# Last stage of a graph network block on one core: another order of gates, shared layer and expert outputs, roots as a power on GpSimd, stores from SP

## The chip, the cores and the metric

The kernel runs on one core of a Trainium2 chip. The time is device microseconds of that core for one whole execution. The core's engines are TensorE (PE in the profile, its weight loads PEld), VectorE (DVE), ScalarE (ACT), GpSimd (POOL) and SP, which here only issues DMAs. Each engine works through its own list of instructions in order; semaphores are the only order between them. TensorE has a granted clock of two levels, 1.2 and 2.4 GHz (0.50 and 1.00 in the profile).

## The reference, cut to what matters

There are 6250 nodes with 256 values and 206250 edges. `xn` is the layer norm of x. A transformer convolution over the edges (8 heads) gives `out`; what follows is per node, and is what the changed stage computes:

```
x_r  = xn @ Wskip.T + bskip
beta = sigmoid(concat[out, x_r, out - x_r] @ Wbeta.T)
y    = layernorm(xn + beta * x_r + (1 - beta) * out) * g1 + b1'
t    = x + layernorm(y + gelu(y @ W1.T + b1) @ W2.T + b2) * g2 + b2'     # W1: 256 -> 1024
m    = layernorm(t)
shared = relu(relu(m @ sW1 + sb1) @ sW2 + sb2) @ sW3 + sb3               # 256, 128, 256
expert_e = relu(relu(m @ eW1 + eb1) @ eW2 + eb2) @ eW3 + eb3             # 4 experts: 128, 64, 256
w    = softmax over the two largest of softmax(m @ gW + gb), else 0
result = t + shared + sum_e w_e * expert_e
```

Everything is fp32. A layer norm divides by sqrt(var + 1e-5).

## The kernel before, in words

Two stages come ahead: projections of all nodes, and the long loop over the edges (until about 2848 us). The diff touches only the last stage, from line 997 on.

**Tiling.** The nodes are 49 blocks of 128 rows. They go through the stage in 13 parts: part 0 has three blocks, parts 1 to 11 have four, part 12 has two (`parts`, `wd`; NS is 13). Hidden layers are computed with features on the partitions and up to 512 nodes as columns (`hidden`, into two PSUM buffers `hid`, which ScalarE empties with gelu or relu). What must come back with nodes on the partitions is computed block by block (`node_major`, 256 columns, into three PSUM buffers `nat`, which VectorE empties). Transposes of the node rows (`transpose_rows`) go through two PSUM buffers `tr`, which ScalarE copies to `rT`.

**Steps.** TensorE's list is a loop over steps s, written out by hand. In step s it does, before the change: W1 of part s (eight `hidden`, and between the fifth and the sixth the transposes of m of part s-1), gate logits and first shared layer of part s-1, W2 of part s, then of part s-1 the first expert layers (e1), the second shared layer (s2) and the second expert layers (e2), the transposes of y of part s+1 and of x of part s+2, the outputs of part s-1 (per block one shared and four expert `node_major`), and `skip` of part s+2. The buffers `hid`, `nat` and `tr` are used in turn, so every engine must take them in the same order; the list `order` numbers them.

**VectorE's list in step s:** `after_attention(s+1)` (the sum for beta, then the sigmoid, first layer norm, y), `gates(s-1)`, `divide_by_sum(s+2)`, `add_ffn(s)` (takes W2's blocks), `after_ffn(s)` (two layer norms; gives t and m, in `mb`), `combine(s-1)` (takes the outputs, five operations per block), `skip_less_out(s+2)` (takes the skip blocks).

**ScalarE's list in step s:** the eight gelus of W1, with exp(-z) of part s+1 behind the third, the copies of the transposes of m behind the fifth, and one root behind the sixth; relus of the first shared layer; two exponentials of the gates; relus of e1 with one root behind the second; s2, e2; copies of the transposes of y and x; one root. A root is exp(-0.5 * ln(var + eps)), two activations of one column per block, each with a load of its function table.

**Other queues.** SP loads `xnb` three parts ahead and `xb` one part ahead, each behind the semaphore that says that the buffer is free. GpSimd issues the stores of `accb` when `combine` is done; the next `combine` waits for the store.

In VectorE's `layernorm` (L1195 to L1207) the statistics are followed by `var_ready`, then a wait for two signals of ScalarE (`rstd_ready`), then the scaling on L1205. Lines in the profile: L1447 is the matmul in `hidden`, L1454 that in `node_major`, L1438 a transpose, L1480 the gate logits; L1385 the activations of hidden layers, L1374 and L1376 the two of a root, L1367 exp(-z), L1380 the gates' exponentials; on VectorE L1198 batch statistics, L1225 `skip_less_out`, L1234 to L1254 `after_attention` (L1234 its first product, L1239 the first operation behind exp(-z)), L1262 `add_ffn`, L1284 the first and L1290 the first operation behind an exponential in `gates`, L1321 and L1326 `combine`.

Of the kernel before, what the change touches and what calls it, by code (L numbers as in the profile page):

```python
# [45 lines left out]
def build(nc, a, out):  # L46
# [75 lines left out]
    with top:  # L122
# [875 lines left out]
        with ExitStack() as s3:  # L998

            W = 4
# [12 lines left out]
            tb = [sbt(s3, f"tb{i}", [P, W, D]) for i in range(2)]  # L1015
# [29 lines left out]
            eps3 = sbt(s3, "eps3", [P, 1])  # L1045
# [5 lines left out]
            lv3 = sbt(s3, "lv3", [P, W])  # L1051
            rs3 = sbt(s3, "rs3", [P, W])
            zb = sbt(s3, "zb", [P, W])
# [7 lines left out]
            we = sbt(s3, "we", [P, W, NE])  # L1061
# [10 lines left out]
            for s in range(NS + 1):  # L1072
                order += [("w1", s), ("r2", s - 1), ("s1", s - 1), ("w2", s), ("e1", s - 1), ("s2", s - 1), ("e2", s - 1),
                          ("r1", s + 1), ("r0", s + 2), ("out", s - 1), ("skip", s + 2)]
# [12 lines left out]
            ws_landed, w3_landed, consts3, rows_set = sem("ws_landed"), sem("w3_landed"), sem("consts3"), sem("rows_set")  # L1087
# [10 lines left out]
            with nc.Block() as block:  # L1098
                @block.sync
                def _(sp):  # L1100
# [39 lines left out]

                    for dst, src in loads[:NW3S]:
                        sp.dma_start(dst, src).then_inc(ws_landed, 16)
# [32 lines left out]
                def _(dve):  # L1175
# [414 lines left out]
```

## Time and profile before

| | us |
|---|---|
| median of three runs (3913.5 to 3918.82) | 3915.66 |
| the profiled execution | 3916.25 |
| its span, first to last instruction | 3914.2 |
| of the span, the last stage | from about 2848 on |
| TensorE busy over the span | 3539.5 (90%) |
| VectorE, ScalarE, GpSimd busy | 1990.8, 1675.7, 2048.3 |

The profile is one execution. A timeline row has the start and the time of one or several like instructions on one engine, its source line, the operation, the tile written and those read, and in brackets the idle time ahead of it with what ended it. An fp32 matmul shows as two records on PE. Ends of matmuls are modelled, so a start minus the next start is the better measure. A row of the busy table gives a stretch and its length, then for PE, PEld, DVE, ACT and POOL the busy us with the number of instructions, then the granted clock, the share of the DMA engines and GB/s. A stage's time on the path is read from TensorE's starts; busy shares over the whole span mix three stages with different limits.

### The profile page before, as it was taken

The page shows a single profiled execution, that of the slowest core. Times are in us where ns is not written, and L with a number is a line of the kernel's source. Part 1 is how long each engine was busy: PE and PEld are TensorE (multiplying, and loading weights), DVE is VectorE, ACT ScalarE, POOL GpSimd, SP SyncE. Part 2 cuts the span into 40 slices and gives each one's busy share as a digit, 9 for nine tenths or more (in the row PEclk, how much of TensorE's full clock was granted, in tenths as well). Part 3 has the DMA queues.
Part 4 walks back from the last instruction along what each step waited for, and adds up shares of the span by engine and source line. Part 5 has one row for each costly group of instructions (what it writes and reads, how often), then busy time and mean ns, then how long its engine had stood idle before and what let it go on. Part 6 is the DMA issues. An engine that isn't in the chain of part 4 may idle for free. (4 is left out here: it accounts for less than half of the span.)

```text
span 3914.2 us, 77635 instructions
## 1 busy us (share of the span) xinstructions
PE 3539.5 (90%) x22914; PEld 2185.8 (56%) x22914; DVE 1990.8 (51%) x5550; ACT 1675.7 (43%) x3636; POOL 2048.3 (52%) x2100
## 2 busy tenths in 40 slices
PE   5879999999999999999999999999948898898988
PEld 2445555555555555555555555555535555555645
DVE  6344444544454554454554454454456555555553
ACT  2234444444444444444444444444424434334342
POOL 3067777777777777777777777777700000000000
PEclk9979999999999999999999999999978888888887
DMA  6467777777777777777777777777620000000000
GB/s 206 162 162 197 192 194 196 198 196 195 195 197 195 196 196 198 197 196 197 198 202 194 195 196 194 198 196 198 159 77 21 22 17 22 17 22 20 11 14 14
DMA packets 637776, 572.41 MB, mean 146 GB/s; under 512 B 430486, under 2 KB 523991, under 8 KB 637700
## 3 DMA queue, kind: packets, MB, share of 16 engines
q0 software_dynamic: 159616, 429.57, 37.1%
q1 hardware_dynamic: 478100, 142.10, 17.3%
q8 instruction: 30, 0.49, 0.1%
q14 instruction: 30, 0.25, 0.0%
HBM read 632.99 MB, written 33.05 MB: 170 GB/s over the span
## 5 line engine op out<-in xcount | busy, mean ns | idle before, releaser
L610 POOL DMA_INDIRECT F<-kv_rows,srcg x1970 | 1996.6, 1014 | 689.0 <-issue 595.9
L686 DVE COPY PT<-pPT 128x384 f32<-128x384 f32 x393 | 219.2, 558 | 1139.6 <-PE pPT L876 1137.3
L883 PE MATMUL pZ<-F,PT 128*64 128x320 f32 x4704 | 744.7, 435 | 0.0
L856 PE MATMUL ring<-ident,F 128*128 128x128 f32 x3940 | 605.3, 285 | 130.6 <-ACT FT L788 122.1
L856 PEld LDWEIGHTS ring<-ident,F 128*128 128x128 f32 x3940 | 418.6, 141 | 417.4 <-ACT FT L788 215.1
L788 ACT ACTIVATE FT<-ring 128x512 f32<-128x512 f32 (+1 forms) x1182 | 579.1, 525 | 68.2 <-PE ring L856 10.3
L794 ACT ACTIVATE Pw<-pS,nMn 128x384 f32<-128x384 f32 x393 | 226.8, 577 | 870.8 <-DVE nMn L681 832.9
L1168 POOL DMA_DIRECT2D out_dram<-accb x13 | 9.8, 750 | 1046.5 <-DVEq L1330 1046.5
L883 PEld LDWEIGHTS pZ<-F,PT 128*64 128x64 f32 x4704 | 368.4, 136 | 253.7 <-issue 1.8
L869 PE MATMUL pS<-F,G 80*64 80x320 f32 x1572 | 299.4, 459 | 0.0
L866 PE MATMUL pS<-FT,qh 128*32 128x320 f32 x3144 | 294.1, 446 | 1.2 <-issue 0.7
L674 DVE TENSOR_SCALAR F<-F,nid 16x640 f32<-16x640 int32 x394 | 245.1, 622 | 19.2 <-issue 1.3
L680 DVE TENSOR_REDUCE nmx<-pS 128x1 f32<-128x384 f32 x393 | 219.2, 558 | 56.8 <-PE pS L869 50.7
L832 ACT ACTIVATE Zs<-pZ 128x320 f32<-128x320 f32 x392 | 171.3, 437 | 170.4 <-PE pZ L883 163.2
L1454 PE MATMUL nat<-eW,e 65*128 65x256 f32 x392 | 168.0, 598 | 63.2 <-DVE accb L1321 63.2
L896 PE MATMUL pZv<-ident,Zs 128*128 128x64 f32 x1568 | 218.2, 262 | 0.0
L876 PE MATMUL pPT<-ident,Pw 128*128 128x128 f32 x1179 | 215.4, 292 | 0.8 <-ACT Pw L794 0.8
L889 PE MATMUL pM<-ident,F 64*128 64x64 f32 x1965 | 206.3, 233 | 0.0
L896 PEld LDWEIGHTS pZv<-ident,Zs 128*128 128x128 f32 x1568 | 205.9, 192 | 0.0
L1385 ACT ACTIVATE h<-hid,b1c 128x512 f32<-128x512 f32 (+2 forms) x104 | 66.2, 661 | 299.8 <-PE hid L1447 299.5
L869 PEld LDWEIGHTS pS<-F,G 80*64 80x64 f32 x1572 | 77.9, 135 | 204.8 <-issue 204.8
L806 ACT ACTIVATE G<-pM 64x512 f32<-64x512 f32 x99 | 58.5, 591 | 310.9 <-PE pM L846 310.9
(214 smaller groups left out, 4477.8 us busy)
## 6 DMA issues: line engine op xcount, KB each, us to landing
F<-in_edge_attrT SPq DMA_DIRECT2D x788, 80.0 KB
F<-kv_rows,srcg POOLq DMA_INDIRECT x1970
F<-in_dst SPq DMA_DIRECT2D x788, 20.0 KB
srci<-src_front SPq DMA_DIRECT2D x796, 1.5 KB, 3.2
kv_rows<-kvs SPq DMA_DIRECT2D x7, 1792.0 KB, 6.7
qb<-q_cols SPq DMA_DIRECT2D x100, 64.0 KB
U<-in_x SPq DMA_DIRECT2D x7, 896.0 KB, 10.9
xn_rows<-xs SPq DMA_DIRECT2D x7, 896.0 KB, 6.7
```

The source lines that it names most:

```text
L610: pool.indirect_dma_start(out=F[s][:, t, 0:KV], out_offset=None, in_=kv_d, in_offset=bass.IndirectOffsetOnAxis(ap=srcg[j % GB][:, col:col ...
L674: dve.tensor_scalar(F3[j][DE:K3, :], F3[j][DE:K3, :].bitcast(I32), nid[DE:K3, c], None, ALU.not_equal).then_inc(neq_done, 1)
L680: ch.step(dve.tensor_reduce(nmx[:, j:j + 1], pS[:, 0:SW], AX.X, ALU.max, negate=True))
L686: dve.tensor_copy(PT[:, :, :], pPT[:, 0:SW].rearrange("p (t r) -> p t r", r=P)).then_inc(pt_emptied, 1)
L788: act.activation(FT[j % 2][:, :, t0 * P:t1 * P], ring[n % 2][:, 0:KD * w].rearrange("p (k e) -> p k e", e=w), ACT.Copy).then_inc(ring_empt ...
L794: act.activation(Pw[:, :], pS[:, 0:SW], ACT.Exp, bias=nMn[:, j:j + 1], accum_out=lsum[:, j:j + 1]).then_inc(p_done, 1)
L856: m = pe.transpose(ring[n % 2][:, k * w + (t - t0) * P:k * w + (t - t0 + 1) * P], F[j][:, t, k * P:(k + 1) * P], ident[:, :])
L866: pe.matmul(pS[r:r + C, o * HP:o * HP + OW], qh[half][:, c, g + o, :], FT[j % 2][:, c, o * OW:(o + 1) * OW], start=True, stop=False)
L869: m = pe.matmul(pS[o * HP:(o + 1) * HP, o * HP:o * HP + OW], G3[half][0:K3, g + o, :, :].rearrange("p c r -> p (c r)"), F3[s][0:K3, o * OW ...
L876: m = pe.transpose(pPT[:, t * P:(t + 1) * P], Pw[:, t * P:(t + 1) * P], ident[:, :])
L883: m = pe.matmul(pZ[rows, 0:ZW], PT[:, t, rows], F[s][:, o * TO + t, D:FP], start=(t == 0), stop=(t == KB - 1))
L896: pe.matmul(pZv[:, g].rearrange("p (o c r) -> p o c r", o=2, c=KD)[:, :, c, :], Zs[:, c * P:(c + 1) * P], ident[:, :].rearrange("p (o c r) ...
```

## The change

- TensorE's step becomes: W1 of part s with the transposes of m of part s-1 inside, gate logits and first shared layer of part s-1, W2 of part s, transposes of y (s+1) and x (s+2), **outputs of part s-2**, `skip` (s+2), and then e1, s2, e2 of part s-1. There are NS + 2 steps in place of NS + 1.
- VectorE: `gate_sum`, the first half of `after_attention`, becomes a function of its own and moves behind `skip_less_out`; `combine(s-2)` stands behind `add_ffn(s)`; `after_ffn(s)` moves to the end of the step. Each `layernorm` gets one more operation, var + eps.
- The roots are one `tensor_tensor` with `ALU.pow` and a tile of -0.5 on GpSimd. ScalarE has no roots any more, and exp(-z) moves to the end of its step.
- The stores are issued by SP, between the loads of `xnb` and `xb`.
- `tb` has three buffers in place of two, `we` two in place of one.

```diff
@@ -1069,9 +1069,9 @@
             tr_at, hid_at, nat_at = {}, {}, {}
             nt = nh = nn = 0
             order = [("r0", 0), ("skip", 0), ("r0", 1), ("skip", 1), ("r1", 0)]
-            for s in range(NS + 1):
-                order += [("w1", s), ("r2", s - 1), ("s1", s - 1), ("w2", s), ("e1", s - 1), ("s2", s - 1), ("e2", s - 1),
-                          ("r1", s + 1), ("r0", s + 2), ("out", s - 1), ("skip", s + 2)]
+            for s in range(NS + 2):
+                order += [("w1", s), ("r2", s - 1), ("s1", s - 1), ("w2", s), ("r1", s + 1), ("r0", s + 2), ("out", s - 2),
+                          ("skip", s + 2), ("e1", s - 1), ("s2", s - 1), ("e2", s - 1)]
             for name, p in order:
                 if 0 <= p < NS:
                     if name in ("r0", "r1", "r2"):
...
@@ -1138,6 +1139,21 @@
                             sp.wait_ge(x_used, p)
                         sp.dma_start(xb[:, 0:t1 - t0, :], x_d[:, t0:t1, :]).then_inc(xb_landed, 16)
 
+                    stored = [0]
+
+                    def store(p):
+                        t0, t1 = parts[p]
+                        sp.wait_ge(out_ready, p + 1)
+                        whole = min(t1, N // P) - t0
+                        last = min(t1 * P, N) - (t0 + whole) * P
+                        if whole:
+                            stored[0] += 1
+                            sp.dma_start(out[t0 * P:(t0 + whole) * P, :].rearrange("(j p) d -> p j d", p=P), accb[:, 0:whole, :]
+                                         ).then_inc(out_stored, 16)
+                        if last:
+                            stored[0] += 1
+                            sp.dma_start(out[(t0 + whole) * P:N, :], accb[0:last, whole, :]).then_inc(out_stored, 16)
+
                     for dst, src in loads[:NW3S]:
                         sp.dma_start(dst, src).then_inc(ws_landed, 16)
                     load_xn(0)
@@ -1146,36 +1162,43 @@
                         sp.dma_start(dst, src).then_inc(w3_landed, 16)
                     load_x(0)
                     load_xn(2)
-                    for s in range(NS):
+                    for s in range(NS + 2):
                         if s + 3 < NS:
                             load_xn(s + 3)
+                        if s >= 2:
+                            store(s - 2)
                         if s + 1 < NS:
                             load_x(s + 1)
+                    sp.wait_ge(out_stored, 16 * stored[0])
 
                 @block.gpsimd
                 def _(pool):
                     pool.memset(tri[:, :, :], 1.0).then_inc(consts3, 1)
                     pool.wait_ge(consts3, 1)
+                    pool.memset(half[:, :], -0.5).then_inc(half_set, 1)
+                    pool.wait_ge(half_set, 1)
 
                     pool.affine_select(out=tri[:, :, :], in_=tri[:, :, :], compare_op=ALU.is_ge, fill=0.0, base=-1,
                                        pattern=[[1, NE], [-1, NE]], channel_multiplier=0).then_inc(consts3, 1)
 
-                    for p, (t0, t1) in enumerate(parts):
-                        pool.wait_ge(out_ready, p + 1)
-                        whole = min(t1, N // P) - t0
-                        last = min(t1 * P, N) - (t0 + whole) * P
-                        if whole:
-                            pool.dma_start(out[t0 * P:(t0 + whole) * P, :].rearrange("(j p) d -> p j d", p=P), accb[:, 0:whole, :]
-                                           ).then_inc(out_stored, 16)
-                        if last:
-                            pool.dma_start(out[(t0 + whole) * P:N, :], accb[0:last, whole, :]).then_inc(out_stored, 16)
-                    pool.wait_ge(out_stored, 16 * (NS - 1 + (whole > 0) + (last > 0)))
+                    lns = [0]
+
+                    def rstd(p):
+                        lns[0] += 1
+                        pool.wait_ge(var_ready, lns[0])
+                        pool.tensor_tensor(rs3[:, 0:wd[p]], vr3[:, 0:wd[p]], half[:, 0:wd[p]], ALU.pow).then_inc(rstd_ready, 1)
+
+                    rstd(0)
+                    for s in range(NS):
+                        if s + 1 < NS:
+                            rstd(s + 1)
+                        rstd(s)
+                        rstd(s)
 
                 @block.vector
                 def _(dve):
                     ch = Chain(dve, "dve3")
 
-                    dve.memset(eps3[:, :], LN_EPS).then_inc(rows_set, 1)
                     dve.memset(e2[EH2:EH2 + 1, :, :], 1.0).then_inc(rows_set, 1)
                     dve.wait_ge(ws_landed, 16 * NW3S)
                     dve.wait_ge(consts3, 2)
@@ -1198,9 +1221,10 @@
                             s = dve.bn_stats(st3[:, j, :], src[:, j, :])
                         ch.step(s)
                         mean_and_var(dve, ch, st3[:, 0:w, :], mn3[:, 0:w], vr3[:, 0:w], D)
+                        ch.step(dve.tensor_scalar(vr3[:, 0:w], vr3[:, 0:w], LN_EPS, None, ALU.add))
                         dve.sem_inc(var_ready, 1)
                         lns[0] += 1
-                        dve.wait_ge(rstd_ready, 2 * lns[0])
+                        dve.wait_ge(rstd_ready, lns[0])
                         for j in range(w):
                             s = dve.tensor_scalar(dst[:, j, :], src[:, j, :], mn3[:, j:j + 1], rs3[:, j:j + 1],
                                                   ALU.subtract, ALU.mult)
@@ -1225,16 +1249,22 @@
                             dve.tensor_sub(d[:, j, :], nat[n % NATS][:, 0:D], d[:, j, :]).then_inc(nat_emptied, 1)
                         dve.wait_ge(nat_emptied, nat_at["skip", p] + wd[p])
 
-                    def after_attention(p):
+                    def gate_sum(p):
 
                         w, d = wd[p], db[p % 3]
-                        ob, x, t, y = weighted(p)[:, :, :, 0:C], xnb[p % 2], ta[:, 0:w, :], yb[:, 0:w, :]
+                        ob, t, y = weighted(p)[:, :, :, 0:C], ta[:, 0:w, :], yb[:, 0:w, :]
                         if p >= 1:
                             dve.wait_ge(tr_filled, tr_at[1, p - 1] + wd[p - 1])
                         ch.step(dve.tensor_tensor(heads(t), ob, heads(wide(w12, w)), ALU.mult))
                         ch.step(dve.tensor_tensor(y, d[:, 0:w, :], wide(w23, w), ALU.mult))
                         ch.step(dve.tensor_add(t, t, y))
                         dve.tensor_reduce(zb[:, 0:w], t, AX.X, ALU.add).then_inc(z_ready, 1)
+                        dve.wait_ge(z_ready, p + 1)
+
+                    def after_attention(p):
+
+                        w, d = wd[p], db[p % 3]
+                        ob, x, t, y = weighted(p)[:, :, :, 0:C], xnb[p % 2], ta[:, 0:w, :], yb[:, 0:w, :]
                         dve.wait_ge(ez_ready, p + 1)
                         ch.step(dve.tensor_scalar(ezb[:, 0:w], ezb[:, 0:w], 1.0, None, ALU.add))
                         ch.step(dve.reciprocal(ezb[:, 0:w], ezb[:, 0:w]))
...
@@ -1331,28 +1361,31 @@
 
                     divide_by_sum(0)
                     skip_less_out(0)
+                    gate_sum(0)
                     after_attention(0)
                     divide_by_sum(1)
                     skip_less_out(1)
-                    for s in range(NS + 1):
+                    gate_sum(1)
+                    for s in range(NS + 2):
                         if s + 1 < NS:
                             after_attention(s + 1)
-                        if s >= 1:
+                        if 1 <= s <= NS:
                             gates(s - 1)
                         if s + 2 < NS:
                             divide_by_sum(s + 2)
                         if s < NS:
                             add_ffn(s)
-                            after_ffn(s)
-                        if s >= 1:
-                            combine(s - 1)
+                        if s >= 2:
+                            combine(s - 2)
                         if s + 2 < NS:
                             skip_less_out(s + 2)
+                            gate_sum(s + 2)
+                        if s < NS:
+                            after_ffn(s)
 
                 @block.scalar
                 def _(act):
-                    act.wait_ge(rows_set, 2)
-                    lns = [0]
+                    act.wait_ge(rows_set, 1)
 
                     def transposed(r, p):
 
...
@@ -1385,49 +1409,42 @@
                         act.activation(dst[0:rws, k, 0:w], hid[n % 2][0:rws, 0:w], func, bias=bias[0:rws, k:k + 1]).then_inc(hid_emptied, 1)
 
                     transposed(0, 0)
+                    exp_z(0)
                     transposed(0, 1)
-                    exp_z(0)
-                    rstd(0)
                     transposed(1, 0)
+                    exp_z(1)
                     act.wait_ge(w3_landed, 16 * (NW3 - NW3S))
                     for s in range(NS + 1):
                         c = s - 1
                         if s < NS:
                             for k in range(KH):
                                 hidden("w1", s, k, h1, ACT.Gelu, b1c)
-                                if k == 2 and s + 1 < NS:
-                                    exp_z(s + 1)
                                 if k == 4 and c >= 0:
                                     transposed(2, c)
-                                if k == 5 and s + 1 < NS:
-                                    rstd(s + 1)
-                        elif c >= 0:
+                        else:
                             transposed(2, c)
                         if c >= 0:
                             for k in range(KD):
                                 hidden("s1", c, k, sh1, ACT.Relu, sb1c)
                             exp_gates(c, 0)
                             exp_gates(c, 1)
-                            for e in range(NE):
-                                hidden("e1", c, e, e1, ACT.Relu, eb1c)
-                                if e == 1 and s < NS:
-                                    rstd(s)
-                            hidden("s2", c, 0, sh2[:, None, :], ACT.Relu, sb2c)
-                            for e in range(NE):
-                                hidden("e2", c, e, e2, ACT.Relu, eb2c, EH2)
-                        elif s < NS:
-                            rstd(s)
                         if s + 1 < NS:
                             transposed(1, s + 1)
                         if s + 2 < NS:
                             transposed(0, s + 2)
-                        if s < NS:
-                            rstd(s)
+                        if c >= 0:
+                            for e in range(NE):
+                                hidden("e1", c, e, e1, ACT.Relu, eb1c)
+                            hidden("s2", c, 0, sh2[:, None, :], ACT.Relu, sb2c)
+                            for e in range(NE):
+                                hidden("e2", c, e, e2, ACT.Relu, eb2c, EH2)
+                        if s + 2 < NS:
+                            exp_z(s + 2)
 
                 @block.tensor
                 def _(pe):
                     pe.wait_ge(ws_landed, 16 * NW3S)
-                    pe.wait_ge(rows_set, 2)
+                    pe.wait_ge(rows_set, 1)
 
                     def transpose_rows(r, p, src):
                         for j in range(wd[p]):
...
@@ -1507,7 +1524,20 @@
                             pe.wait_ge(hid_emptied, hid_at["w1", s] + KH)
                             for j in range(wd[s]):
                                 node_major(nat_at["w2", s] + j, [(h1[:, k, j * P:(j + 1) * P], W2T[:, k, :]) for k in range(KH)])
-                        if c >= 0:
+                        if s + 1 < NS:
+                            rows_of_y(s + 1)
+                        if s + 2 < NS:
+                            rows_of_x(s + 2)
+                        if o >= 0:
+                            pe.wait_ge(hid_emptied, hid_at["e2", o] + NE)
+                            for j in range(wd[o]):
+                                cols, n = slice(j * P, (j + 1) * P), nat_at["out", o] + j * (1 + NE)
+                                node_major(n, [(sh2[:, cols], sW3[:, :])])
+                                for e in range(NE):
+                                    node_major(n + 1 + e, [(e2[:, e, cols], eW3[:, e, :])])
+                        if s + 2 < NS:
+                            skip(s + 2)
+                        if 0 <= c < NS:
                             for e in range(NE):
                                 hidden("e1", c, e, P, [(eW1[:, i, e, :], rT[2][:, i, 0:wc]) for i in range(KD)])
                             pe.wait_ge(hid_emptied, hid_at["s1", c] + KD)
@@ -1515,19 +1545,6 @@
                             for e in range(NE):
                                 pe.wait_ge(hid_emptied, hid_at["e1", c] + e + 1)
                                 hidden("e2", c, e, EH2, [(eW2[:, e, :], e1[:, e, 0:wc])])
-                        if s + 1 < NS:
-                            rows_of_y(s + 1)
-                        if s + 2 < NS:
-                            rows_of_x(s + 2)
-                        if c >= 0:
-                            pe.wait_ge(hid_emptied, hid_at["e2", c] + NE)
-                            for j in range(wd[c]):
-                                cols, n = slice(j * P, (j + 1) * P), nat_at["out", c] + j * (1 + NE)
-                                node_major(n, [(sh2[:, cols], sW3[:, :])])
-                                for e in range(NE):
-                                    node_major(n + 1 + e, [(e2[:, e, cols], eW3[:, e, :])])
-                        if s + 2 < NS:
-                            skip(s + 2)
 
 
 NW3, NW3S = 26, 10

```

## Rows read from the trace of the kernel before

**Rows 1.** Busy table of the last stage: from:to, length, each engine's busy us (instructions), clock.

```profile
2900.00:3914.00 1014.00, 878.18 (x2794) 562.45 (x2792) 569.02 (x1385) 403.53 (x635) 10.36 (x14) 0.85 0.06 18
```

**Rows 2.** Timeline of TensorE over one full step: start, us, engine, line, what.

```profile
3186.76 8.75 PE L1447 MATMUL hid<-rT,W1T 128*128 128x512 f32 x20
...
3197.77 5.32 PE L1447 MATMUL hid<-rT,W1T 128*128 128x512 f32 x12
...
3202.93 1.84 PE L1480 MATMUL pg<-gW,rT 128*128 128x4 f32 x16
...
3205.56 5.40 PE L1447 MATMUL hid<-rT,sW 128*128 128x512 f32 x8 [0.79 <-ACT h L1385]
...
3210.79 13.98 PE L1454 MATMUL nat<-W2T,h 128*128 128x256 f32 x64
...
3224.61 7.03 PE L1447 MATMUL hid<-rT,eW 128*128 128x512 f32 x16
...
3232.78 1.95 PE L1447 MATMUL hid<-sh,sW 128*128 128x512 f32 x4 [1.14 <-ACT e L1385]
...
3238.48 0.66 PE L1438 MATMUL tr<-ident,yb 128*128 128x128 f32 x4
...
3242.03 0.60 PE L1454 MATMUL nat<-sW,sh 128*128 128x256 f32 x2
...
3248.92 2.08 PE L1454 MATMUL nat<-eW,e 65*128 65x256 f32 x4 [5.44 <-DVE accb L1321]
...
3263.59 5.36 PE L1454 MATMUL nat<-WskT,rT 128*128 128x256 f32 x16
...
3268.78 3.60 PE L1447 MATMUL hid<-rT,W1T 128*128 128x512 f32 x8
```

**Rows 3.** Timeline of VectorE in the same step and the next.

```profile
3213.24 0.17 DVE L1290 TENSOR_REDUCE gs<-gx 128x4 f32<-128x16 f32 x1 [3.92 <-ACT gx L1380]
...
3219.99 0.76 DVE L1262 TENSOR_TENSOR tb<-nat,db 128x256 f32<-128x256 f32 x2
...
3225.26 1.40 DVE L1198 BATCH_NORM_STATS2 st<-tb 128x6 f32<-128x256 f32 x4
...
3232.09 1.38 DVE L1205 TENSOR_SCALAR db<-tb,mn,rs 128x256 f32<-128x256 f32 x4 [4.01 <-ACT rs L1376]
...
3245.77 1.38 DVE L1205 TENSOR_SCALAR mb<-tb,mn,rs 128x256 f32<-128x256 f32 x4 [5.57 <-ACT rs L1376]
...
3269.44 1.23 DVE L1234 TENSOR_TENSOR ta<-U,w 128x1024 f32<-128x1024 f32 x1
...
3276.37 0.17 DVE L1239 TENSOR_SCALAR ezb<-ezb 128x4 f32<-128x4 f32 x1 [1.93 <-ACT ezb L1367]
...
3285.56 1.38 DVE L1205 TENSOR_SCALAR db<-ta,mn,rs 128x256 f32<-128x256 f32 x4 [2.88 <-ACT rs L1376]
...
3290.76 0.17 DVE L1284 TENSOR_TENSOR g<-pg,rows 128x16 f32<-128x16 f32 x1
```

**Rows 4.** Busy table of two stretches inside expert outputs.

```profile
3252.00:3256.00 4.00, 4.00 (x11) 3.12 (x10) 2.25 (x5) 0.00 (x0) 0.00 (x0) 0.50 0.00 0
...
3904.00:3909.00 5.00, 4.70 (x20) 2.97 (x19) 4.14 (x9) 0.00 (x0) 0.00 (x0) 1.00 0.00 0
```

**Rows 5.** Timeline of VectorE in the outputs of the last part.

```profile
3905.04 2.04 DVE L1326 SCALAR_TENSOR_TENSOR accb<-nat,we,accb 128x256 f32<-128x256 f32 x4
```

**Rows 6.** GpSimd's groups of instructions over the whole span.

```profile
L315 POOL MEMSET U<- 128x1848 f32 x7 | 11.3, 1638 | 57.0 <-DVE xs L354 56.5 <-POOL posb L309 0.5
...
L283 POOL TENSOR_SCALAR_AFFINE_SELECT selh<-selh 128x4 f32<-128x4 f32 x32 | 6.1, 190 | 5.0 <-POOL selh L283 0.5
```

**Rows 7.** Timeline of TensorE, W1 of parts 0, 2 and 11.

```profile
2898.85 2.82 PE L1447 MATMUL hid<-rT,W1T 128*128 128x384 f32 x8 [0.57 <-ACT rT L1362]
...
3022.30 8.75 PE L1447 MATMUL hid<-rT,W1T 128*128 128x512 f32 x20
...
3757.73 9.19 PE L1447 MATMUL hid<-rT,W1T 128*128 128x512 f32 x20
```

More of the change, by code:

```diff
@@ L1014, in build @@
             db = [sbt(s3, f"db{i}", [P, W, D]) for i in range(3)]
-            tb = [sbt(s3, f"tb{i}", [P, W, D]) for i in range(2)]
+            tb = [sbt(s3, f"tb{i}", [P, W, D]) for i in range(3)]
             yb = sbt(s3, "yb", [P, W, D])
@@ L1050, in build @@
             vr3 = sbt(s3, "vr3", [P, W])
-            lv3 = sbt(s3, "lv3", [P, W])
             rs3 = sbt(s3, "rs3", [P, W])
+            half = sbt(s3, "half", [P, W])
             zb = sbt(s3, "zb", [P, W])
@@ L1060, in build @@
             rank = sbt(s3, "rank", [P, W, NE])
-            we = sbt(s3, "we", [P, W, NE])
+            we = [sbt(s3, f"we{i}", [P, W, NE]) for i in range(2)]
             NATS = 3
@@ L1085, in build @@
                         nh += {"w1": KH, "s1": KD, "s2": 1, "e1": NE, "e2": NE}[name]
-            ws_landed, w3_landed, consts3, rows_set = sem("ws_landed"), sem("w3_landed"), sem("consts3"), sem("rows_set")
+            ws_landed, w3_landed, consts3, rows_set, half_set = (
+                sem("ws_landed"), sem("w3_landed"), sem("consts3"), sem("rows_set"), sem("half_set"))
             xn_landed = [sem(f"xn_landed3{i}") for i in range(2)]
@@ L1256, in add_ffn @@
                     def add_ffn(p):
-                        d, t = db[p % 3], tb[p % 2]
+                        d, t = db[p % 3], tb[p % 3]
                         for j in range(wd[p]):
@@ L1265, in after_ffn @@
                     def after_ffn(p):
-                        w, dd, tt = wd[p], db[p % 3], tb[p % 2]
+                        w, dd, tt = wd[p], db[p % 3], tb[p % 3]
                         d, t = dd[:, 0:w, :], tt[:, 0:w, :]
@@ L1307, in gates @@
                         dve.wait_ge(ge_ready, 2 * p + 2)
-                        ch.step(dve.tensor_tensor(we[:, tt, :], gx[:, tt, :], rank[:, tt, :], ALU.mult))
-                        ch.step(dve.tensor_reduce(gs[:, tt], we[:, tt, :], AX.X, ALU.add))
+                        ch.step(dve.tensor_tensor(we[p % 2][:, tt, :], gx[:, tt, :], rank[:, tt, :], ALU.mult))
+                        ch.step(dve.tensor_reduce(gs[:, tt], we[p % 2][:, tt, :], AX.X, ALU.add))
                         ch.step(dve.reciprocal(gs[:, tt], gs[:, tt]))
-                        ch.step(dve.tensor_tensor(we[:, tt, :], we[:, tt, :], four(gs), ALU.mult))
+                        ch.step(dve.tensor_tensor(we[p % 2][:, tt, :], we[p % 2][:, tt, :], four(gs), ALU.mult))
                     def combine(p):
-                        t = tb[p % 2]
+                        t = tb[p % 3]
                         if p >= 1:
@@ L1489, in _ @@
                     pe.wait_ge(w3_landed, 16 * (NW3 - NW3S))
-                    for s in range(NS + 1):
-                        c = s - 1
+                    for s in range(NS + 2):
+                        c, o = s - 1, s - 2
                         if s < NS:
@@ L1498, in _ @@
                                     rows_of_m(c)
-                        elif c >= 0:
+                        elif c < NS:
                             rows_of_m(c)
-                        if c >= 0:
+                        if 0 <= c < NS:
                             wc = wd[c] * P
@@ L1509, in _ @@
                                 node_major(nat_at["w2", s] + j, [(h1[:, k, j * P:(j + 1) * P], W2T[:, k, :]) for k in range(KH)])
-                        if c >= 0:
+                        if s + 1 < NS:
[11 more added lines that the diff above has]
+                            skip(s + 2)
+                        if 0 <= c < NS:
                             for e in range(NE):
```

11 lines of the change are left out of this document (1 added, 10 removed).

## Prediction, made before the kernel after was run

> **What bounds the kernel now.** I read the busy shares by stretch first, then TensorE's timeline of one step of the last stage, then VectorE's beside it, then the granted clock. The change leaves everything up to 2848 us alone; the last stage is the 1014 us of [rows 1], with TensorE busy 878 us of it at a mean granted clock of 0.85. So there are two losses: waits, and time at 1.2 GHz. [Rows 2] are TensorE's starts in one full step. W1 of the next step begins 3268.78 - 3186.76 = 82.0 us after W1 of this one. The largest wait is 5.44 us before the second expert output: PSUM buffers come free only when `combine` starts, and `combine` stands on VectorE behind the whole of `after_ffn`, which itself waited 4.01 and 5.57 us for ScalarE's roots [rows 3]. After that gap the clock is 0.50 although TensorE is busy 4.00 of 4.00 us [rows 4], and stays there through the outputs into `skip`: from 3248.92 to 3263.59 us 14.7 us for outputs whose matmuls take half of that at 2.4 GHz. TensorE is the engine that binds; the chain of a step runs over it, with VectorE and ScalarE only at the gaps.
>
> **The change on TensorE.** I rebuild a step from its starts, all at the full clock. One fp32 matmul shows as two records; a W1 record takes (3202.93 - 3197.77)/12 = 0.43 us, a W2 record (3224.61 - 3210.79)/64 = 0.216 us [rows 2].
> - W1: 32 x 0.43 = 13.8. Gate logits 1.84. First shared layer 8 x 0.43 = 3.4 (5.23 now: half of it ran at half clock, after 2.6 us of gate logits and idling). W2 13.8.
> - Transposes of y and x: 3242.03 - 3238.48 = 3.55 for 8 tiles; those of m, 4 tiles at that rate, 1.8.
> - e1, s2, e2: 3238.48 - 3224.61 = 13.9, less the 1.14 us wait for ScalarE, which stood on two table loads for a root; these go. 12.7.
> - Outputs: VectorE limits them at full clock. The last part shows it: four weighted sums in 2.04 us [rows 5] and one addition of about 0.4, 2.46 per block, 9.8 for four.
> - `skip`: 16 records x 0.216 = 3.5.
> Sum 64.2 us. No matmul is added or dropped: the same parts pass through once, in 15 steps instead of 14. I add 1.0 us, half of the 1.8 us that the first shared layer loses when the clock falls ahead of it; it may still fall there in some steps. 65.2 against 82.0.
>
> **Does VectorE keep up?** Its order becomes: rest of `after_attention`, gates, `divide_by_sum`, `add_ffn`, `combine` (two parts back), `skip_less_out`, `gate_sum`, `after_ffn`. What was never on the path is now near it: `m_ready`. Let 0 be the end of `skip` on TensorE and X the time from variance to root on GpSimd, both handoffs included. `gate_sum` begins at 0.66 and takes 4 x 1.26 = 5.0. `after_ffn` took 3245.77 - 3225.26 = 20.5 us to its last scaling, 9.6 of it the two waits [rows 3]; with that scaling (1.4) and two added eps additions (0.2 each) it is 12.7 + 2X. So m is ready at 18.4 + 2X. TensorE asks for it after e1 to e2 and five eighths of W1, at 12.7 + 8.6 = 21.3. It is in time while X is below 1.5.
> Then one 1.26 addition, `after_attention` (3290.76 - 3276.37 = 14.4, less its 2.88 wait, plus 0.2 = 11.7, plus X): gates start at 31.4 + 3X. They need the exponentials, which came 3213.24 - 3210.79 = 2.45 us after the first shared layer ended; that end is now at 12.7 + 13.8 + 1.8 + 1.8 + 3.4 = 33.5, so 36.0; from there to the first W2 addition 3219.99 - 3213.24 = 6.75, and 0.45 for it: 43.2. TensorE needs this buffer for the fourth W2 block at 33.5 + 10.4 = 43.9. Also in time, with 0.7 us to spare. `combine` finds VectorE free when the outputs begin. Both margins are thin, both hang on X.
>
> **X.** No row shows a power on GpSimd. From below: its small one-input operations take 0.19 us [rows 6], with two handoffs some 0.3. From above: the largest computing operation of GpSimd there is 1.64 us for 1848 columns [rows 6]; the wait that is removed was 2.88 to 5.57 with table loads [rows 3], and a root could be dearer than either. I take 1.0 for four columns, nearer to the small rows, and keep 0.3 to about 7 as bounds. The Trainium skill (GPSIMD Engine Reference, Performance versus the Vector engine) puts a two-input operation at 1.96 times VectorE's; by it this one would be some 0.35 us, an estimate, but the page prices an addition, not a power. The same page (Instruction dispatch) says that the first call of newly loaded code costs about 6 us: that would make 3723 of the time below; no row here shows it.
>
> **The other parts.** ScalarE: three roots a step, each with two loads of its table, leave it; the loads that remain stand beside TensorE. exp(-z) moves to the end of a step, where z has been ready since `gate_sum`: nothing waits. It also stands no longer in W1, so the transposes of m find ScalarE free. SP: a store takes POOL's place, behind the load of xn (asked for at the start of the step) and ahead of the load of x, whose buffer comes free only after `after_ffn`, later than `combine`: the store delays nothing, and the next `combine` asks for it a whole step later. These cost nothing; if a store did hold the x load, a step of slack is there. The third `tb` and second `we` only hold values longer.
>
> **Ends of the stage.** Head, W1 of part 0 to W1 of part 2: 3022.30 - 2898.85 = 123.5 now [rows 7]. New: W1, W2, transposes, skip for three blocks and for four, and part 0's layers (by the numbers above, three quarters for three blocks; no outputs yet) are 77.4; plus 5 for ScalarE, which now waits for z of part 1 before its first gelu; plus 8 for m of part 0 (TensorE gets there after only 8.6 us of W1, VectorE needs 5.0 + 9.7 + 2X = 16.7); plus 4 for the half clock behind that. 94.4; gain 29, most of it the first outputs, which come later. Middle, steps 2 to 10: 3757.73 - 3022.30 = 735.4 now; new 9 x 65.2 = 586.8, less 2.5 (outputs of a part of three blocks), less 2.6 (part 12 has two), plus 2.3 (m late once): 584.0; gain 151. Tail: 3914.2 - 3757.73 = 156.5 now; new 58.1 (step 11, little to transpose or skip) + 43.4 (step 12) + 24.8 (step 13: 19.8 of work and 5 for the last gates ahead of `combine`) + 4.9 (last outputs) + 4.7 (store, as now) + 2 = 137.9; gain 19.
> Together 199: span 3914.2 - 199 = 3715. The profiled execution took 3916.25 us, 2.0 more than its span, and the three runs have a median of 3915.66; I forecast 3717.
>
> **Rivals.**
> A, the clock stays at 1.2 GHz in the outputs. Ahead of them stand transposes in bursts, and at full clock TensorE pauses at each output for VectorE (0.43 of work in 0.5). If it falls there, it stays, as it did although TensorE was fully busy [rows 4]: 14.7 + 2.1 for the first two against 9.8, some 7.2 per step, 87 in all: 3804. Against it: the last part's outputs ran at 1.00 throughout, paused by VectorE in just this way [rows 4, 5]. The page TensorE: Matmul & The Clock Gate of the Trainium skill (A second HAM failure mode) says that small idles between groups, as PSUM banks are cycled, make the clock oscillate: that speaks for A. The same page (Part 1) has sustained activity release the throttle, by which the outputs now should not have stayed slow; the measurement decides, they did.
> B, the root costs 1.5 to 5 us. At 3 us m is 3.1 late and the W2 buffer another 1.5: 4.6 per step, 55 in all, some more in the head: 3775.
> C, slower than before: the same root, dearer. At X = 7 m is 11.1 late, the buffer (39.5 + 3X against 43.9 plus that wait) another 5.5, and an idle of this length leaves the last three eighths of W1 at half clock, 12 x 0.43 = 5.2 more: 87.0 per step, 5.0 over now, about 3975. It decides from X = 5.7. For it: GpSimd computes almost nothing in this kernel, so nothing bounds it from its own rows; against: four columns.
> D, the order does not do what it says: the outputs find their buffers free, but another handoff that I hold for hidden (x copies, y) takes the wait, and only the roots' loads and a few us a step are won: 3850.
>
> **How the numbers follow.** Forecast 0.55, A 0.15, B 0.19, C 0.05, D 0.06. The range 3685 to 3805 takes in the forecast, B and A; its lower end is mine without the additions of 1.0 per step and half of the head's waits. A change within 0.2% (8 us) is what a measurement cannot tell from none; only between C and D does it fall there, 0.01. Faster 0.94, slower 0.05.
>
> **What would show it.** W1 starts 64 to 66 us apart, no gap of 5 us before the outputs, granted clock near 1.0 in them, 2.5 us per block; transposes of m without a wait of more than 0.5 us; GpSimd's power under 1.2 us. It is wrong if TensorE waits for `mb`, if the output blocks take 4.27 us, or if the W2 blocks wait for VectorE.

## The result and the profile after

The kernel after took 3708.0 us (3707.56 to 3708.03, three runs) against 3915.66: 0.947 of before, 95% interval 0.945 to 0.949. Its profiled execution has a span of 3705.8 us. The forecast was 3717 in a range of 3685 to 3805. Two of the sets of runs below were taken while the stage over the edges took some 1000 us more in every kernel (the kernel before: medians of 5019 and 4975 us, mean granted clock 0.83 in place of 0.95); the kernels in them are compared by the length of the last stage in their profiles, first transposes of x to the end, which is 1046.0 us before and 836.9 after.

TensorE's timeline of one full step, in the columns of [rows 2]:

```profile
3185.22 8.83 PE L1464 MATMUL hid<-rT,W1T 128*128 128x512 f32 x20
3193.88 0.60 PE L1455 MATMUL tr<-ident,mb 128*128 128x128 f32 x4
3195.10 0.71 PE L1455 MATMUL tr<-ident,mb 128*128 128x128 f32 x4 [0.61 <-ACT rT L1395]
3195.65 5.32 PE L1464 MATMUL hid<-rT,W1T 128*128 128x512 f32 x12
3200.80 1.84 PE L1497 MATMUL pg<-gW,rT 128*128 128x4 f32 x16
3202.50 3.68 PE L1464 MATMUL hid<-rT,sW 128*128 128x512 f32 x8
3206.02 13.98 PE L1471 MATMUL nat<-W2T,h 128*128 128x256 f32 x64
3219.83 0.60 PE L1455 MATMUL tr<-ident,yb 128*128 128x128 f32 x4
...
3223.12 0.60 PE L1471 MATMUL nat<-sW,sh 128*128 128x256 f32 x2
...
3232.69 3.69 PE L1471 MATMUL nat<-WskT,rT 128*128 128x256 f32 x16
3236.22 7.03 PE L1464 MATMUL hid<-rT,eW 128*128 128x512 f32 x16
...
3248.74 8.82 PE L1464 MATMUL hid<-rT,W1T 128*128 128x512 f32 x20
```

From W1 to W1 it is 3248.74 - 3185.22 = 63.5 us, against 82.0 in [rows 2]. The 5.44 us ahead of the outputs are gone, the first shared layer takes 3206.02 - 3202.50 = 3.5 in place of 5.2, and the outputs 3232.69 - 3223.12 = 9.6. Before they took 3263.59 - 3242.03 = 21.6 with the gap, 14.7 of it behind the gap at half clock. VectorE and GpSimd beside it:

```profile
3191.04 1.01 POOL L1189 TENSOR_TENSOR rs<-vr,half 128x4 f32<-128x4 f32 x1 [8.49 <-DVEq L1225]
```

```profile
3192.09 1.38 DVE L1229 TENSOR_SCALAR mb<-tb,mn,rs 128x256 f32<-128x256 f32 x4 [1.18 <-POOL rs L1189]
...
3215.27 0.76 DVE L1292 TENSOR_TENSOR tb<-nat,db 128x256 f32<-128x256 f32 x2
```

A root costs VectorE 1.18 us where it waited 5.57 for the same one in [rows 3]. (The 5.57 were not all roots: the variance was ready at 3240.2, and ScalarE, still busy with copies of transposes, began the root's first table load at 3242.63.) m is ready at 3192.09 + 1.38 = 3193.47 us and TensorE takes it at 3193.88: 0.4 us of margin. The busy table answers to [rows 1] and [rows 4]: the whole last stage, a stretch in the outputs of a full step, and one in the last outputs but one.

```profile
2900.00:3705.00 805.00, 765.43 (x2789) 472.30 (x2788) 570.95 (x1422) 247.37 (x448) 37.02 (x38) 0.98 0.07 22
3224.00:3232.00 8.00, 8.00 (x35) 5.21 (x33) 7.54 (x17) 0.00 (x0) 0.00 (x0) 1.00 0.00 0
3674.00:3682.00 8.00, 8.00 (x22) 6.13 (x21) 4.91 (x12) 0.00 (x0) 0.00 (x0) 0.55 0.00 1
```

TensorE was busy 878 of 1014 us at 0.85 and is now busy 765 of 805 us at 0.98: the matmuls are the same, so the 113 us less of busy time went with the clock, and the other 96 are waits. The third row is read below, at the ends of the stage.

### The profile page after: what moved, and what is told of

Its sections match the earlier page's. It is cut to its first block and busy times, and to the rows that moved or that the text cites. A ratio compares the mean times of both kernels' runs of the same rounds, so it can differ in the third digit from the quotient of the medians.

```text
span 3705.8 us, 77538 instructions
## 1 busy us (share of the span) xinstructions
PE 3428.3 (93%) x22914; PEld 2096.6 (57%) x22914; DVE 1991.6 (54%) x5588; ACT 1514.8 (41%) x3445; POOL 2058.8 (56%) x2126
## 5 line engine op out<-in xcount | busy, mean ns | idle before, releaser
L1189 POOL TENSOR_TENSOR rs<-vr,half 128x4 f32<-128x4 f32 (+2 forms) x39 | 37.9, 972 | 769.7 <-DVEq L1225 769.7
L680 DVE TENSOR_REDUCE nmx<-pS 128x1 f32<-128x384 f32 x393 | 219.0, 557 | 54.2 <-PE pS L869 42.6
L1464 PE MATMUL hid<-rT,W1T 128*128 128x512 f32 (+2 forms) x416 | 181.2, 589 | 9.5 <-ACT h L1409 8.9
L889 PEld LDWEIGHTS pM<-ident,F 64*128 64x128 f32 x1965 | 152.2, 139 | 66.3 <-issue 66.3
```

The source lines that it names most:

```text
L889: m = pe.transpose(pM[:, t * DE:(t + 1) * DE], F3[s][0:DE, t * P:(t + 1) * P], ident[0:DE, 0:DE])
L1464: m = pe.matmul(hid[n % 2][0:rws, 0:w], l, r, start=(q == 0), stop=(q == len(terms) - 1))
```

## The experiments

The theory that the prediction carried, T1: the order makes the gain. The rival T2: the roots make it, since `after_ffn` becomes shorter by more than the gap. Two kernels take one of the two each; both have the stores from SP. They were run in the set at 5019 us and once more where the stage over the edges took its usual time. Two profiles of the same kernel agree on the last stage within 1.8 us (858.7 and 860.5, roots alone) and 4.8 us (998.0 and 993.2, order alone), so a few us in a single profile decide nothing by themselves.

**The roots alone, old order.** The edit, beside the stores from SP:

```diff
+                        pool.tensor_tensor(rs3[:, 0:wd[p]], vr3[:, 0:wd[p]], half[:, 0:wd[p]], ALU.pow).then_inc(rstd_ready, 1)
...
-                        act.activation(lv3[:, w], vr3[:, w], ACT.Ln, bias=eps3[:, 0:1]).then_inc(rstd_ready, 1)
-                        act.wait_ge(rstd_ready, 2 * lns[0] - 1)
-                        act.activation(rs3[:, w], lv3[:, w], ACT.Exp, scale=-0.5).then_inc(rstd_ready, 1)
```

> The old order of all engines, with only the roots on GpSimd and the stores from SP. Theory T1 (the order makes the gain, as the prediction's step was built): the expert outputs still stand behind the whole of after_ffn, a wait of some us stays ahead of them and the clock still falls; a step keeps at least 75 us, the time 3840 or more. Rival T2 (the roots alone do it): after_ffn loses its 9.6 us of waits on ScalarE and gets 2.4 on GpSimd, so combine starts 16.9 us after W2 ends, and TensorE reaches its fourth output only 17.6 us after it: no gap, no fall of the clock, a step of 65.1 us (64.2 and 0.9 for exp(-z), which still delays the transposes of m), about 3720 to 3730.

> The same kernel as old_order_pow, to get its time from more rounds. By the traces its last stage is 858.7 us against 1046.0 of the kernel before: 187 us, so 3728 where the kernel before takes 3916 (ratio 0.952), wherever the stage over the edges takes the same time. A ratio above 0.97 in that case would say that the trace of one execution was no good guide.

With the usual stage over the edges it took 3729.49 us against 3917.1 of the kernel before, 0.952 (95% interval 0.951 to 0.953); in the set at 5019 us the ratio was 0.956 (0.943 to 0.968). A step is 64.6 us where T2 said 65.1. TensorE, then VectorE:

```profile
3196.54 8.75 PE L1464 MATMUL hid<-rT,W1T 128*128 128x512 f32 x20
...
3206.99 0.71 PE L1455 MATMUL tr<-ident,mb 128*128 128x128 f32 x4 [1.28 <-ACT rT L1388]
...
3247.77 0.60 PE L1471 MATMUL nat<-sW,sh 128*128 128x256 f32 x2
3248.21 2.24 PE L1471 MATMUL nat<-eW,e 65*128 65x256 f32 x8
...
3257.58 3.69 PE L1471 MATMUL nat<-WskT,rT 128*128 128x256 f32 x16
3261.11 1.45 PE L1464 MATMUL hid<-rT,W1T 128*128 128x512 f32 x3
```

```profile
3246.07 1.38 DVE L1231 TENSOR_SCALAR mb<-tb,mn,rs 128x256 f32<-128x256 f32 x4 [1.18 <-POOL rs L1190]
...
3248.74 0.42 DVE L1347 TENSOR_TENSOR accb<-nat,tb 128x256 f32<-128x256 f32 x1
```

`combine` still stands behind all of `after_ffn`, and it still begins in time: 3248.74 us, 1.0 us behind the first output matmul, just as the third buffer is filled. No gap, and the clock stays at 1.00. T1 expected 3840 or more and fell; T2's 3720 to 3730 holds. The roots alone are 188 us of the 208. Of the 82.0 - 64.6 = 17.4 us per step, 13.4 are the gap, the outputs and `skip` behind it; the other 4.0 are gained where a root on ScalarE stood in TensorE's way: 0.9 at the gate logits, 1.7 in the first shared layer, 1.4 between e1 and e2. So "the roots" are two things, a shorter wait of VectorE and a free ScalarE. Whether another place for the roots in ScalarE's list would do in the old order was not tried.

**The order alone, roots on ScalarE.**

```diff
                                 hidden("w1", s, k, h1, ACT.Gelu, b1c)
                                 if k == 4 and c >= 0:
+                                    rstd(c)
                                     transposed(2, c)
+                                if k == 7 and s + 1 < NS:
+                                    rstd(s + 1)
...
                             hidden("s2", c, 0, sh2[:, None, :], ACT.Relu, sb2c)
+                            if s < NS:
+                                rstd(s)
```

> The new order, with the roots on ScalarE as before (behind s2, behind the fifth gelu and behind the eighth gelu). T1: most of the gain stays, 3730 or less. T2, with the prediction's own terms for a root of about 3.1 us with its table loads: m comes 5 us late behind five eighths of W1, and the W2 buffer 1 to 3 us late; a step of 70 to 73 us, 3780 to 3820, so this order alone gives about half to two thirds of the gain. The transposes of m wait for mb 4 to 6 us per step.

> The same kernel as new_order_act, to get its time where the stage over the edges is as short as in the first times. Its trace had 998.0 us in the last stage against 1046.0 before: 48 us less, so 3868 (ratio 0.988) by that trace. If the order were what gains, as T1 has it, 3730.

3863.5 us against 3916.38, 0.986 (0.985 to 0.988); in the set at 5019 us 0.989 (0.979 to 0.999). That is far from T1's 3730 or less, and also above T2's 3780 to 3820. A full step is mostly 76.7 to 76.9 us, more than T2's 70 to 73. TensorE's waits of one step, and its outputs:

```profile
3170.52 2.27 PE L1463 MATMUL tr<-ident,mb 128*128 128x128 f32 x8 [5.32 <-DVE mb L1218]
...
3197.01 3.72 PE L1479 MATMUL nat<-W2T,h 128*128 128x256 f32 x16 [1.59 <-DVE tb L1281]
...
3203.85 0.60 PE L1479 MATMUL nat<-sW,sh 128*128 128x256 f32 x2
...
3213.42 3.69 PE L1479 MATMUL nat<-WskT,rT 128*128 128x256 f32 x16
...
3230.26 2.83 PE L1472 MATMUL hid<-e,eW 128*64 128x512 f32 x4 [2.66 <-ACT e L1408]
...
3247.92 2.28 PE L1463 MATMUL tr<-ident,mb 128*128 128x128 f32 x8 [5.32 <-DVE mb L1218]
```

The outputs take 9.6 us without a gap, as in the kernel after. The wait moved from them to m (5.3 us, as expected), the W2 buffer is 1.6 late (expected 1 to 3), and 2.7 us were not in the sum: the root behind s2 holds the relus of the second expert layer. The waits are 9.6 of the 13.2 us over the kernel after; most of the rest is half clock behind the first and the last of them (the twelve W1 records behind m took 7.1 us in place of 5.2). That last wait belongs to where I placed the root in ScalarE's list; this kernel says what one placement gives, not the best one. The order alone is worth 53 us, and on top of the roots 3729.5 - 3708.0 = 21.5. These are times from different sets; by the profiles the last stage is 21.8 or 23.6 us shorter.

**What a gap costs.** Work of VectorE that nobody needs, three or five products of 1.23 us, ahead of each `combine` in the old order with roots on GpSimd:

```diff
                         if s >= 1:
+                            for _ in range(3):
+                                ch.step(dve.tensor_tensor(scr[:, :, :], scr[:, :, :], scr[:, :, :], ALU.mult))
                             combine(s - 1)
```

> The old order with roots on GpSimd, and three products of 1.23 us on a tile that nobody reads ahead of each combine on VectorE. If the clock answers to the length of the gap: TensorE waits about 3.5 us ahead of the fourth output; a gap of 3.18 us was followed by half clock in step 13 of the kernel after. Clock theory (outputs stay at 1.2 GHz once it has fallen): 65.1 + 3.5 + up to 7.2, 72 to 76 us per step, more than the gap itself. Rival (a wait costs only its own length): 68.6 us per step, about 3765.

> As before with five such products, 6.2 us of VectorE. Clock theory: a gap of about 5.5 us as in the kernel before, and the outputs at half clock behind it: about 65.1 + 5.5 + 7.2 = 78 us per step, about 3870. Rival (the wait costs only itself): 70.6 us, about 3790.

The timeline and the busy table of the outputs, first with three, then with five:

```profile
4507.92 2.07 PE L1475 MATMUL nat<-eW,e 65*128 65x256 f32 x4 [3.78 <-DVE accb L1349]
```

```profile
4509.00:4522.00 13.00, 13.00 (x32) 10.31 (x31) 7.08 (x15) 0.00 (x0) 0.00 (x0) 0.50 0.00 0
```

```profile
4517.66 2.07 PE L1475 MATMUL nat<-eW,e 65*128 65x256 f32 x4 [6.31 <-DVE accb L1349]
...
4532.32 5.01 PE L1475 MATMUL nat<-WskT,rT 128*128 128x256 f32 x16
```

```profile
4518.00:4532.00 14.00, 14.00 (x34) 11.04 (x34) 7.91 (x18) 0.00 (x0) 0.00 (x0) 0.50 0.00 1
```

The full steps are 75.5 to 77.1 us, mean 76.1, and 78.5, against 64.6 without: 11.5 and 13.9 more. The last stages are 978.2 and 1007.9 us. The expectation that a wait costs only its own length (68.6 and 70.6) fell; the other (72 to 76, and 78) holds. Less the gaps of 3.8 and 6.3 that leaves 7.7 and 7.6 us, the same for both: the outputs and the start of `skip` at half clock. TensorE is fully busy in both stretches and the clock stays at 0.50. A gap of 3.8 us costs 11.5.

**A dearer root.** Each power is computed four or seven times, in the kernel after:

```diff
+                        for _ in range(3):
+                            pool.tensor_tensor(rs3[:, 0:wd[p]], vr3[:, 0:wd[p]], half[:, 0:wd[p]], ALU.pow).then_inc(again, 1)
+                            n_again[0] += 1
+                            pool.wait_ge(again, n_again[0])
                         pool.tensor_tensor(rs3[:, 0:wd[p]], vr3[:, 0:wd[p]], half[:, 0:wd[p]], ALU.pow).then_inc(rstd_ready, 1)
```

> The kernel after with each power computed four times in a row on GpSimd, so a root takes 1.2 + 3 x 1.05 = about 4.4 us. By the prediction's terms m comes 2 x 4.4 + 18.4 - 21.3 = 5.9 us late and the W2 buffer another 3.0: 72 us per step without a fall of the clock, 77 with it in the rest of W1: 3810 to 3870. Rival (GpSimd's time is hidden as everything else was): 3715.

> Each power seven times, a root of about 7.5 us. Prediction's terms: m 12.1 us late, the buffer another 5.9, half clock 5.2 behind the gap: 87 us per step, 3970 to 4000, slower than the kernel before; rival C of the prediction said that the point where it becomes slower is at 5.7. If only two thirds of that are right, 3890.

With four the step is 72.8 us, with seven 85.3; the last stage 950.2 and 1089.1 us, the latter longer than the 1046.0 of before (ratio of whole times 1.008, 1.006 to 1.011). VectorE and TensorE with four, the clock just behind the gap and a little later, then the same engines with seven:

```profile
4429.26 1.38 DVE L1233 TENSOR_SCALAR mb<-tb,mn,rs 128x256 f32<-128x256 f32 x4 [4.44 <-POOL rs L1193]
```

```profile
4430.69 2.28 PE L1459 MATMUL tr<-ident,mb 128*128 128x128 f32 x8 [6.01 <-DVE mb L1233]
4432.77 7.26 PE L1468 MATMUL hid<-rT,W1T 128*128 128x512 f32 x12
```

```profile
4431.00:4436.00 5.00, 4.95 (x12) 2.51 (x11) 4.72 (x10) 1.54 (x4) 0.00 (x0) 0.50 0.00 0
4437.00:4444.00 7.00, 7.00 (x30) 4.12 (x29) 2.32 (x12) 1.92 (x4) 4.03 (x4) 1.00 0.21 70
```

```profile
4703.54 1.38 DVE L1233 TENSOR_SCALAR mb<-tb,mn,rs 128x256 f32<-128x256 f32 x4 [7.70 <-POOL rs L1193]
```

```profile
4704.98 2.28 PE L1459 MATMUL tr<-ident,mb 128*128 128x128 f32 x8 [12.52 <-DVE mb L1233]
...
4733.73 6.48 PE L1475 MATMUL nat<-W2T,h 128*128 128x256 f32 x16 [4.99 <-DVE tb L1296]
4740.05 0.60 PE L1459 MATMUL tr<-ident,yb 128*128 128x128 f32 x4
```

m is 6.0 and 12.5 us late where 5.9 and 12.1 were expected. The W2 buffer is 1.7 us late with four, where 3.0 was expected, and 5.0 with seven, where 5.9 was. Behind the wait for m the clock is back before the end of W1: the last twelve records took 6.0 us in one step and 7.1 in the next, 5.9 with seven, in place of 5.2, so 0.8 to 1.9 us are lost and not the 5.2 that I had put down. With seven, half clock also stands behind the second wait, which I had not put down: 16 records of W2 take 4740.05 - 4733.73 = 6.3 us in place of 3.5. The step of 85.3 is below the 87 expected.

**The stores from GpSimd again.** The same calls, moved back from SP's list to GpSimd's, between its roots.

> The kernel after with the stores issued by GpSimd again, between its roots. Both theories: no change, 3706 to 3712; a store takes GpSimd 0.75 us at a moment when no root is asked for. A rival, that the queue matters (a store's issue delays the next root by more than the 0.4 us that m has to spare): 3715 to 3725.

The last stage takes 836.3 us, against 836.9, and a step 63.5; the whole 0.962 of before (0.953 to 0.971), too wide to say more. GpSimd's list of one step:

```profile
4316.23 1.01 POOL L1171 TENSOR_TENSOR rs<-vr,half 128x4 f32<-128x4 f32 x1 [8.49 <-DVEq L1226]
4326.58 1.01 POOL L1171 TENSOR_TENSOR rs<-vr,half 128x4 f32<-128x4 f32 x1 [9.35 <-DVEq L1226]
4359.10 0.79 POOL L1183 DMA_DIRECT2D out_dram<-accb  x1 [31.51 <-DVEq L1361]
```

The store falls into its long idle time. In the new order it costs nothing on either queue that the profiles show; in the old order this was not tried.

**Other ends of the stage.** The kernel after has one more gap, in step 13, with half clock behind it (0.55 from 3674 to 3682 us, the third row of the busy table above). TensorE:

```profile
3668.83 1.03 PE L1471 MATMUL nat<-eW,e 65*128 65x256 f32 x4
3673.04 1.22 PE L1471 MATMUL nat<-eW,e 65*128 65x256 f32 x4 [3.18 <-DVE accb L1351]
...
3686.53 4.58 PE L1464 MATMUL hid<-rT,eW 128*128 128x256 f32 x16
```

The part of the edit at the tail (the first run also changes the head):

```diff
-                        if 1 <= s <= NS:
+                        if 1 <= s < NS:
                             gates(s - 1)
...
                         if s >= 2:
                             combine(s - 2)
+                        if s == NS:
+                            gates(s - 1)
...
                         elif c < NS:
+                            outs(o)
                             rows_of_m(c)
```

> The kernel after with its two ends put in another order: in step 0 VectorE does after_ffn(0) ahead of gate_sum(2), with exp(-z) of part 2 behind W1 of part 1; in step 13 the outputs of part 11 stand ahead of the transposes of m of part 12, and gates(12) behind combine(11). Expected from the trace: the transposes of m of part 0 come 5 us earlier, the 3.2 us wait and the half clock of the last outputs but one go (14.5 us from 3668.4 to 3686.5 less its 9.8 becomes about 0, against some 5 us of gates that stand bare later): 3708 less 5 and less 5 to 10, so 3693 to 3699. If the clock falls at the other places instead, no gain: 3705.

> The kernel after with only the change at the last steps that new_ends had (outputs of part 11 ahead of the transposes of m of part 12, gates(12) behind combine(11)). The trace of new_ends showed 78.3 us from W1 of part 12 to the end in place of 85.1, and 2.9 us lost at the head. So the last stage should take 836.9 - 6.8 = 830.1 us, the whole 3701 on a chip with the first times (0.998 of the kernel after). If the 6.8 us were luck of the clock, 836.9 again.

With both ends changed the last stage took 833.0 us: 6.8 won in the tail (W1 of part 12 to the end 78.3 in place of 85.1). The head lost 6.0 between W1 of parts 1 and 2 (66.2 in place of 60.2). W1 of part 1 came 3.0 earlier, but so it did in the next kernel, which leaves the head as it was; so the edit of the head costs 6 us (833.0 against 826.8). There m came earlier, as expected, and the W2 blocks of part 1 waited instead:

```profile
4072.45 5.40 PE L1478 MATMUL nat<-W2T,h 128*128 128x256 f32 x16 [8.91 <-DVE tb L1292]
```

With the tail alone: 826.8 us, whole time 3700.49 us (3696.83 to 3701.46), 0.945 of before (0.944 to 0.946). It is the lowest time here, but the interval overlaps that of the kernel after (0.945 to 0.949), and the two were not run side by side; what the edit gives is read from the tail, 78.4 us. The remaining 3 us of the stage are between W1 of parts 0 and 1, 32.6 us here and 35.6 in the kernel after. The kernel with the order alone had 35.6 in one profile and 32.6 in the other, so I don't count them to the edit.

## Why the prediction was right, and what it had wrong

- **The step.** Forecast 64.2 and 1.0 for the clock; measured 63.5. The outputs took 9.6 us of the 9.8 put down, the transposes of m 1.8 of 1.8, and exp(-z) out of W1 left a wait of 0.61 where it had been 1.28. The 0.7 us too many are small terms, mostly transposes, e1 to e2, outputs and gate logits. The 1.0 was not needed: the clock never fell ahead of the first shared layer.
- **Margins.** m at 18.4 + 2X and asked for at 21.3: with X = 1.18 that is 20.8; measured from the end of `skip` (63.5 before 3236.22, so 3172.7) 20.8 and 21.2. The first W2 addition was put at 42.7 and came at 3215.27 - 3172.7 = 42.6. X was taken at 1.0 and measured 1.18, below the 1.5 from which rival B begins. No load of code showed at the first power, which took 0.89 us within a wait of 1.07:

```profile
2885.72 1.06 DVE L1229 TENSOR_SCALAR db<-ta,mn,rs 128x256 f32<-128x256 f32 x3 [1.07 <-POOL rs L1189]
```

The 6 us that the Trainium skill (GPSIMD Engine Reference, Instruction dispatch) gives for the first call of newly loaded code did not appear there.
- **Ends.** Head 94.4 against 95.8 measured. That was in part luck: I had put down 5 for ScalarE and 8 for m, and the rows show 3.9 and 4.4 us behind gelus and 3.4 for m. Middle 584.0 against 570.3: 9 of the difference are the unneeded 1.0 per step and 6 the 0.7 by which the step was too long, less 1.6 that step 2 took longer. Tail 137.9 against 142.2: I had put down the wait for the last gates, not the half clock behind it (the outputs of part 11 took 18.1 us in place of 14.8). The errors partly cancel: 3717 for 3708.
- **Rival A** had the right price, 7.2 against the 7.7 and 7.6 of the two gap kernels, and did not come about: the outputs ran at 1.00 although VectorE paused them. In the full steps small pauses did not bring the clock down (0.48 us per operation of VectorE, clock 1.00). The Trainium skill (TensorE: Matmul & The Clock Gate, A second HAM failure mode) has such pauses make it oscillate; these rows do not bear that out. Sustained work in the outputs did not bring it up (busy 14.00 of 14.00 us, clock 0.50), where the Trainium skill (TensorE: Matmul & The Clock Gate, Part 1: The HAM clock gate) has activity release the throttle; these rows do not bear that out either. But a wait need not be long. In step 10 of the kernel with the roots alone a wait of 0.97 us ahead of the fourth output was followed by half clock, 0.50 from 3574 us on (0.96 and the same fall in its other profile):

```profile
3572.11 1.22 PE L1471 MATMUL nat<-eW,e 65*128 65x256 f32 x4 [0.97 <-DVE accb L1347]
...
3577.23 1.06 PE L1471 MATMUL nat<-sW,sh 128*128 128x256 f32 x2
...
3585.77 3.62 PE L1471 MATMUL nat<-WskT,rT 128*128 128x256 f32 x8
```

That step took 69.8 us, against 60.8 in the kernel after. So A's condition stood closer than the full steps show.
- **Rival C** was real and its formula good (m late by 6.0 and 12.5), but the buffer's term was 1.2 too high (1.7 and 5.0 where X - 1.5 gives 2.9 and 6.2), and the half clock behind the wait for m was mis-sized, 5.2 for 0.8 to 1.9. By VectorE's waits X was 4.44 and 7.70; between 72.8 us and 85.3 there a straight line crosses the old 82.0 at X = 6.8. The prediction's 5.7 is also a slip: its own terms, 65.2 + (2X - 2.9) + (X - 1.5) + 5.2, reach 82 at 5.3.
- **Which edit gains.** This failed. The prediction took the gap for a matter of the order, as `combine` stands behind the whole of `after_ffn`. It put a price on the roots' loads by themselves only in rival D (3850, so 66 us won), and never asked whether they alone would close the gap. Its own rows had it: 9.6 us of `after_ffn` were waits on ScalarE, against a gap of 5.44. The runs show 188 us for the roots alone, 53 for the order alone, 208 for both. They overlap because both take away the same gap. That the whole time came out right says nothing about this step: the kernel after has both edits.

What the order adds on top of the roots is read from the starts of W1 (roots alone against both): part 0 to part 2 107.4 us against 95.8, part 2 to part 11 586.4 against 570.3, from there to the end 138.5 against 142.2. Of the 16 in the middle 7 are steps 2 to 9 (1.05 per full step, 0.7 of it the longer wait in the transposes of m, 1.28 for 0.61), and 9 are step 10 with the wait of 0.97. In the head the old order has a wait of 8.84 us at the first `skip` behind `after_ffn` and a gap of 2.9 ahead of a set of outputs; in the tail it has one of 2.6, and is shorter even so. What each of these is worth by itself was not tried.
